# Storing attention's results by feature, with the reciprocals of their sums, and multiplying the two in the next stage: a decoder layer on one Trainium2 core

## The reference, cut to what matters

```python
# B = 4, S = 512, D = 256, 16 heads of 16, 160 experts, top 8
weights = softmax(einsum('bqhd,bkhd->bhqk', q, k) * 16 ** -0.5)
out = einsum('bhqk,bkhd->bqhd', weights, v)
x = layernorm(x + out.reshape(B, S, D) @ w_o.T)          # attention
x = layernorm(x + cross_attention(x, ctx_1024))          # "the mix"
x = layernorm(x + mixture_of_experts(x))                 # routed + shared expert
```

## Time and profile before

| | |
|---|---|
| median of 3 runs | 1057.27 us |
| the profiled execution | 1051.34 us, of which the span is 1049.5 us |
| attention | 0 to 287 us; its even part, 91.4 to 247.4 us, has PE busy for 154.6 of 156 us, DVE for 122.9, ACT for 110.4 |
| the mix | 287 to some 630 us |
| the experts and the end | some 630 to 1049.5 us |
| granted PE clock | 1.00 of full speed in the even part of attention, 0.83 in 285 to 345 us, 0.85 from 620 us on |
| DMA share | 0.78 in the even part of attention, 0.14 in 285 to 345 us |

### The profile page before, as it was taken

The page is one execution under the profiler, slowest core; times in us unless marked ns, Lnnn a source line. Parts: engine busy times, 40 slices in busy tenths (PEclk is TensorE's granted clock), DMA queues, the critical chain, the costliest instruction groups (busy, mean ns, idle before and its releaser), DMA issues. The chain is left out here.

```text
span 1049.5 us, 14995 instructions
## 1 busy us (share of the span) xinstructions
PE 805.3 (77%) x3800; PEld 533.6 (51%) x3800; DVE 492.6 (47%) x1287; ACT 381.8 (36%) x809; POOL 358.2 (34%) x360
## 2 busy tenths in 40 slices
PE   8989999999778898297484013888888887886295
PEld 4654444444246556174263012666666665765274
DVE  2778778777142576256424941222222222321077
ACT  3256777677623434215111000333333333332101
POOL 9101101110000014536265560555555555554200
PEclk9989999999969989698697555988989999887698
DMA  7998777885511022222122226888898887883296
GB/s 243 317 340 283 262 258 255 265 281 214 190 41 61 20 74 96 107 65 88 44 99 77 71 104 210 263 280 267 283 286 276 277 281 249 269 261 98 78 421 251
DMA packets 103410, 207.45 MB, mean 198 GB/s; under 512 B 25863, under 2 KB 51505, under 8 KB 97088
## 3 DMA queue, kind: packets, MB, share of 16 engines
q1 hardware_dynamic: 64160, 128.94, 37.1%
q10 hardware_dynamic: 24320, 42.74, 12.3%
q0 software_dynamic: 14880, 35.17, 9.2%
HBM read 117.76 MB, written 96.08 MB: 204 GB/s over the span
## 5 line engine op out<-in xcount | busy, mean ns | idle before, releaser
L1735 POOL DMA_INDIRECT contributions<-c_c,e_dest x182 | 177.5, 975 | 186.9 <-ACT c_c L1716 132.2
L1883 POOL DMA_INDIRECT row_pool<-rows,places x128 | 127.9, 999 | 210.8 <-issue 156.6
L1690 DVE COPY e_xt<-e_psx 128x256 f32<-128x256 f32 (+1 forms) x130 | 67.4, 530 | 250.7 <-PE e_psx L1622 106.3
L1636 PE MATMUL e_psg<-e_xt,e_w 128*128 128x64 f32 (+2 forms) x676 | 134.8, 339 | 51.8 <-ACT e_g L1709 40.4
L539 DVE TENSOR_REDUCE a_mx<-a_psS 128x2 f32<-128x1024 f32 x128 | 152.0, 1218 | 30.6 <-PE a_psS L361 30.4
L497 ACT ACTIVATE a_e<-a_psT 128x512 f32<-128x512 f32 x256 | 135.4, 600 | 56.4 <-PE a_psT L391 51.3
L1636 PEld LDWEIGHTS e_psg<-e_xt,e_w 128*128 128x128 f32 x676 | 109.7, 222 | 61.5 <-issue 48.8
L1709 ACT ACTIVATE e_g<-e_psg 128x128 f32<-128x128 f32 (+1 forms) x130 | 42.1, 324 | 243.4 <-PE e_psg L1636 132.3
L1647 PE MATMUL e_psy<-e_w,e_g 128*128 128x256 f32 (+1 forms) x442 | 121.4, 437 | 9.6 <-ACT c_c L1716 6.3
L1716 ACT ACTIVATE c_c<-e_psy,e_weight 128x256 f32<-128x256 f32 x182 | 80.7, 474 | 65.2 <-PE e_psy L1647 25.8
L391 PE MATMUL a_psT<-a_q,a_k 128*128 128x512 f32 x256 | 98.3, 451 | 4.6 <-ACT a_e L497 2.8
(11 more groups left out here) (284 smaller groups left out, 953.2 us busy)
## 6 DMA issues: line engine op xcount, KB each, us to landing
row_pool<-fill SPq DMA_DIRECT2D x32, 1260.0 KB, 7.2
e_w<-w ACTq DMA_DIRECT2D x156, 256.0 KB
rows<-row_pool SPq DMA_DIRECT2D x143, 140.0 KB
c_c<-contributions SPq DMA_DIRECT2D x16, 1024.0 KB, 17.1
a_k<-k_parts SPq DMA_DIRECT2D x64, 128.0 KB, 3.5
rows<-row_pool SPq DMA_DIRECT2D x78, 70.0 KB
a_q<-q_parts SPq DMA_DIRECT2D x32, 128.0 KB, 4.1
a_q<-q_parts SPq DMA_DIRECT2D x64, 64.0 KB, 3.4
```

Of the source, the lines that this page charges most:

```text
L1636: last = nc.tensor.matmul(ps_g(f, n)[:, k * own:(k + 1) * own], W[:, place, c * INTER:(c + 1) * INTER], XT[:, f.slot % XT_RING, at0:at0 + ...
L1690: nc.vector.tensor_copy(XT[:, at.slot % XT_RING, 0:n], ps_x(at, 0, n)).then_inc(xt_done, 1)
L1735: nc.gpsimd.indirect_dma_start(out=contrib, out_offset=bass.IndirectOffsetOnAxis(ap=dest[:, result(f) + k:result(f) + k + 1], axis=0), in_ ...
L1883: nc.gpsimd.indirect_dma_start(out=pool, out_offset=bass.IndirectOffsetOnAxis(ap=place[:, b, t, k:k + 1], axis=0), in_=rows[:, b, t], in_o ...
```

## The change

Attention no longer divides or turns its results. `turn_values`, the semaphores `o_turned` and `divided`, and the tiles `On` and `inv` are gone. DVE takes the reciprocal of the whole of `O` (128 x 512, features and sums alike) into a tile `Oinv`, after its second reduction. SP stores the rows of results of `O` and the rows of reciprocals of `Oinv` separately for each of four heads: eight DMAs of 16 rows of 2 KB in place of one. `O` is now held until these have landed. As bank 1 is free earlier, the banks are dealt anew: `BANK` skips it once, in place of twice, `rescore(6)` waits for the shifts, and the waits on exponentials follow from `BANK`.

```diff
-    BANK = [(k + (k >= 4) + (k >= 6)) % NT for k in range(NE)]
-    BEFORE = [None] * 3 + [0, 2, 3, 4, 5, None, 6, 7, 8, 9, 10, 11, 12]
+    BANK = [(k + (k >= 4)) % NT for k in range(NE)]
+    AFTER = 6
+    LAST_OF = [max(k for k in range(NE) if BANK[k] == n) for n in range(NT)]
+    BEFORE = [max((j for j in range(k) if BANK[j] == BANK[k]), default=None) for k in range(NE)]
+    STORES = 2 * HG
@@ SP, a step
-                    sp.wait_ge(divided, at.n - 2)
-                    cols = slice(g.slot * HG * DH, (g.slot + 1) * HG * DH)
-                    sp.dma_start(od[bass.ds(g.uses() - 1, 1), :, :, cols].rearrange("a p t e -> (a p) t e"),
-                                 On[:].rearrange("p t h e -> p t (h e)")).then_inc(stored, 16)
+                    for part, (src, done) in enumerate(((O, o_copied), (Oinv, inverted))):
+                        sp.wait_ge(done, at.n - 2)
+                        for hh in range(HG):
+                            at0 = 2 * DH * hh + DH * part
+                            sp.dma_start(od[bass.ds(g.uses() - 1, 1), part, g.slot, hh].rearrange("a e q -> (a e) q"),
+                                         src[at0:at0 + DH]).then_inc(stored, 16)
@@ PE
             def rescore(at, k):
-                (k < NT: waits on expd; BEFORE[k] None: waits on divided, or on the shifts)
+                if BEFORE[k] is not None:
+                    pe.wait_ge(expd, at.n * NE + BEFORE[k] + 1)
+                elif at.first():
+                    pe.wait_ge(v_done, B * TT)
+                else:
+                    pe.wait_ge(expd, (at.n - 1) * NE + LAST_OF[BANK[k]] + 1)
+                if k == AFTER and m.within(STEPS):
+                    pe.wait_ge(shifted0, m.n + 1)
+                    pe.wait_ge(shifted1, m.n + 1)
-            def turn_values(at):
-                for t in range(TT):
-                    last = nc.tensor.transpose(psT[:, TURNED, t * P:(t + 1) * P], O[:, t * P:(t + 1) * P], ident[:])
@@ ACT, copy_values
-                    act.wait_ge(o_turned, at.n)
+                    act.wait_ge(stored, 16 * STORES * at.n)
@@ DVE
-            def divide(at):
-                nc.vector.reciprocal(inv[:], o[:, :, :, DH]).then_inc(inverted, 1)
-                nc.vector.tensor_tensor(On[:], o[:, :, :, 0:DH], repeated(inv[:], 3, DH), ALU.mult).then_inc(divided, 1)
+            def invert(at):
+                dve.wait_ge(o_copied, at.n + 1)
+                if not at.first():
+                    dve.wait_ge(stored, 16 * STORES * at.n)
+                nc.vector.reciprocal(Oinv[:], O[:]).then_inc(inverted, 1)
-                    if at.back(3).within(STEPS) and i == 2:
-                        divide(at.back(3))
+                    if at.back(3).within(STEPS) and i == 1:
+                        invert(at.back(3))
```

```diff
     def load_heads(self, sp, o):
-        sp.dma_start(self.O[:], o).then_inc(self.o_in, 16)
+        for to, part in ((self.O[:].rearrange("p t d -> p (t d)").rearrange("p (c q) -> p c q", c=DC), 0), (self.OT[:], 1)):
+            sp.dma_start(to, o[part].rearrange("(c g) h e q -> (g h e) c q", c=DC)).then_inc(self.o_in, 16)
@@ DVE
+            def divide_heads(b):
+                dve.wait_ge(o_in, 32 * (b + 1))
+                for c in range(DC):
+                    nc.vector.tensor_tensor(OT[:, c], heads[:, c], OT[:, c], ALU.mult).then_inc(ot_done, 1)
             def start(b):
+                divide_heads(b)
                 measure_heads(b)
@@ DVE, a step
                 if part_c:
                     keep()
+                if part_a:
+                    divide_heads(n + 1)
                 if part_b:
                     statistics(...)
```

More of the change, by code:

```diff
@@ L275, in step @@
                     prefetch(sp)
-                    sp.wait_ge(stored, 16 * (STEPS - 2))
+                    sp.wait_ge(stored, 16 * STORES * (STEPS - 2))
                     first_heads(sp)
             run(sp, step)
-            sp.wait_ge(stored, 16 * STEPS)
+            sp.wait_ge(stored, 16 * STORES * STEPS)
         @block.gpsimd
@@ L376, in rescore @@
             def rescore(at, k):
[L377 to L383, removed]
+                m = at.back(-1)
+                if BEFORE[k] is not None:
                     pe.wait_ge(expd, at.n * NE + BEFORE[k] + 1)
-                elif g.within(STEPS):
-                    pe.wait_ge(divided, g.n + 1)
-                else:
+                elif at.first():
+                    pe.wait_ge(v_done, B * TT)
+                else:
+                    pe.wait_ge(expd, (at.n - 1) * NE + LAST_OF[BANK[k]] + 1)
+                if k == AFTER and m.within(STEPS):
                     pe.wait_ge(shifted0, m.n + 1)
@@ L404, in weigh @@
                 last.then_inc(weighed, 1)
-            def turn_values(at):
[L407 to L413, removed]
-                for t in range(TT):
-                    last = nc.tensor.transpose(psT[:, TURNED, t * P:(t + 1) * P], O[:, t * P:(t + 1) * P], ident[:])
-                last.then_inc(o_turned, 1)
             def step(at):
@@ L441, in step @@
                         weigh(g, TT - 1)
-                    if ending and i == 2:
-                        turn_values(g)
                     if finishing and i in (3, 5, 7):
@@ L514, in split @@
                                         ALU.subtract).then_inc(lo_done, 1)
-            def divide(at):
-                dve.wait_ge(o_turned, at.n + 1)
+            def invert(at):
+                dve.wait_ge(o_copied, at.n + 1)
                 if not at.first():
-                    dve.wait_ge(stored, 16 * at.n)
-                o = psT[:, TURNED].rearrange("p (t h e) -> p t h e", t=TT, h=HG)
-                nc.vector.reciprocal(inv[:], o[:, :, :, DH]).then_inc(inverted, 1)
-                dve.wait_ge(inverted, at.n + 1)
-                nc.vector.tensor_tensor(On[:], o[:, :, :, 0:DH], repeated(inv[:], 3, DH), ALU.mult).then_inc(divided, 1)
+                    dve.wait_ge(stored, 16 * STORES * at.n)
+                nc.vector.reciprocal(Oinv[:], O[:]).then_inc(inverted, 1)
             def shift(at):
@@ L684, in mix @@
         O, o_in = inputs.O, inputs.o_in
-        OT = sb("m_ot", [P, DC, S])
+        OT, heads = inputs.OT, O[:].rearrange("p t d -> p (t d)").rearrange("p (c q) -> p c q", c=DC)
         X1, X1b = (sb(f"m_{n}", [P, TT, D]) for n in ("x1", "x1b"))
@@ L750, in load_a @@
             def load_a(b):
[L752 removed]
+                sp.wait_ge(projected, TT * b)
                 inputs.load_heads(sp, od[b])
[L754 removed]
                 sp.dma_start(X[:], x[b]).then_inc(x_in, 16)
@@ L827, in turn @@
                 last.then_inc(done, 1)
-            def turn_heads(b):
-                pe.wait_ge(o_in, b * 16 + 16)
-                turn(O, 0, o_turned)
             def project_heads(b):
-                pe.wait_ge(ot_done, b + 1)
+                pe.wait_ge(ot_done, DC * (b + 1))
                 pe.wait_ge(x_in, b * 16 + 16)
@@ L964, in step @@
                 for t in range(TT):
-                    if t == 1 and part_a:
-                        turn_heads(n + 1)
                     nc.tensor.matmul(h[:, t], ident, X1b[:, t], start=True, stop=False)
@@ L1000, in _ @@
             w2, w3 = Cols[:, 0:DC], Cols[:, DC:2 * DC]
-            def copy_heads(b):
-                act.wait_ge(o_turned, b + 1)
-                for c in range(DC):
-                    last = nc.scalar.activation(OT[:, c], ps[:, c], ACT.Copy)
-                last.then_inc(ot_done, 1)
             def copy_x1(b):
@@ L1861, in decoder_layer @@
     qd, kd = (dram(n, [STEPS // 2, 2, DH, HG, 2, S]) for n in ("q_parts", "k_parts"))
-    od = dram("o_heads", [B, P, TT, D])
+    od = dram("o_heads", [B, 2, NG, HG, DH, S])
     pool = dram("row_pool", [POOL_ROWS, ROW])
```

14 lines of the change are left out of this document (4 added, 10 removed).

## The result

The changed kernel takes 1093.47 us (median of 4 runs, 1092.63 to 1096.54), the kernel before in the same comparison 1057.12 us (1056.08 to 1058.54). The ratio is 1.035, 95% interval 1.033 to 1.037: slower by 36 us. The forecast was 1108 us, in a range of 1075 to 1134.

The account below looks back on a forecast made before the run. PE was taken to pace attention, DVE having a fifth of its time spare. Attention's 48 us, plus 6 for the seam, less 2.6 in the mix, made 51 us on 1057.3: 1108 us, range 1075 to 1134.

Parts of the forecast that it names:

- The bound and the place: Attention: DVE's reciprocal ahead of six reductions delays score 4, leaving PE idle at least 2.4 us a step.
- The law of the step: Attention: a step grows by the reciprocal's time less 1.5 us, once that is above 1.5; 2.5 us expected.
- The size of R: Attention, DVE: the 512-element reciprocal's duration, taken as 4.0 us, with bounds of 0.69 and 7.8 us.
- the prediction's slow case: Whole kernel: reciprocal of 3.4 to 5.0 us and clock loss of 0 to 2 us a step, 1088 to 1132 us.
- The rival on the faster side: Attention and mix: reciprocal fast and stores hidden, 7.5 and 2.6 us won, seam costs 3: 1050 us; chance 0.13.
- The clock: Attention: idle PE brings a 3.5 us stretch at the lower clock, costing 1.2 us a step; bounds 0 and 2.5.
- The rival in which the clock holds: Attention: PE's gaps don't lower the clock, 32.5 us lost in place of 48: 1093 us; chance 0.13.
- The stores: Attention, SP: seven more stores at 0.65 us add some 4.6 us, 14.1 in all, hidden in a 17.8 us step.
- The second rival: Attention, SP: fast reciprocal, eight stores make SP the bound, steps of 14.1 to 16.2 us, 1057 to 1085 us; chance 0.12.
- The seam: Attention's end to the mix's first projection: 4 us later start plus 3 for multiplications, less 1 gained: 6 us.
- a wait put at nothing: Attention, ACT: its wait for eight stores, issued the step before and landing in some 2.4 us, costs nothing.
- The mix and what follows: Mix's other batches: eight transpositions leave PE's path three times, 0.87 us each, winning 2.6 us.

Follow-up runs that it names:

- v_one: Changed kernel with the reciprocals moved from attention to the mix, one 256 KB store a step and 16 loads a batch: 896.36 us, ratio 0.981 to the kernel before.
- v_r512: v_one with an unread reciprocal of 512 columns put back into each attention step behind the second reduction: 1072.82 us, ratio 1.021 to the kernel before.
- v_r384: v_one with an unread reciprocal of 384 columns put back into each attention step: steps of 15.12 us, ratio 1.000 to the kernel before.
- after_again: The changed kernel run once more, unaltered, beside other variants: 1089.13 us, ratio 1.035 to the kernel before.
- v_eight: v_one with the changed kernel's eight 32 KB stores a step and its two loads a batch: 916.17 us, ratio 1.002 to the kernel before.
- v_issue: v_one with seven more stores a step, each of one 2 KB row that nothing reads: 909.76 us, 11.0 above v_one.
- a_last: Changed kernel with separate tiles for the last group's results and reciprocals, so its copy waits for no store: 1087.78 us beside 1089.13 of after_again.
- v_r256: v_one with an unread reciprocal of 256 columns put back into each attention step: steps of 14.32 us, ratio 0.990 to the kernel before.

## Why the prediction was right, and where it was off

**The bound and the place.** "It is the place of the reciprocal, ahead of six reductions, that hurts, before its sum does": PE's idle bracket in a step is at score 4, released by L524 (L539 of the kernel before), as written. v_one, without the reciprocal, keeps PE busy for 107.99 of 110 us, and v_r512 brings the bracket back alone. The transpositions that went were worth 0.47 us a step there, 0.58 in the prediction.

**The law of the step.** "Longer by R - 1.5 us": with the measured R of 3.34 it gives 14.14 + 1.84 = 15.98, and 15.92 was measured at full clock. The three sizes give the same law: 1.74 - (14.32 - 14.14) = 1.56 us are free against the kernel before, and 2.54 and 3.34 us give 1.56 too.

**The size of R** was the term that missed most: 4.0 us were taken, 3.34 measured, 6.5 ns an element. The line through the earlier trace rows had 7.2 ns; pieces of 128, 256, 384 and 512 columns (926, 1736, 2536 and 3337 ns) give 6.3. Thirteen times 0.66 are 8.6 us; attention's 48 us became 40.2. R even lies below the 3.4 to 5.0 us that the prediction's slow case was spanned with; its lower end, 1088 us, doesn't come out of its own terms either (13 x 1.9 + 6 - 2.6 is 28 us, which gives 1085). The Trainium skill's VectorE: DVE Perf Modes, section "First, the fixed hardware budget", read as eight cycles an element, gives an estimate of 4.3 us. The trace has 3.34, nearer to that than to 0.7 us, the estimate from one element a cycle, which is a reading of Vector Engine (DVE) Microarchitecture Reference, section "3.2 Anatomy of a single slice". The rival on the faster side stood on that reading.

**The clock.** 1.2 us a step were taken, from a stretch of 3.5 us; 1.36 us were measured, in ten steps of twelve, over such a stretch. The rival in which the clock holds gave 1093 us, the time that came out, but the trace refutes it: the clock fell, and that its number was met is luck, as other terms were smaller. In v_r384, with gaps of 1.00 to 1.09 us, the clock did hold.

**The stores.** An issue cost 0.47 us, not 0.65 (four take 1.93 and 1.84 us, on SP's timeline), and they were hidden under the long step, as the prediction said; v_r512 against after_again shows it. The second rival's mechanism is real, but decides only with a short reciprocal: it was v_eight's 20 us. The Trainium skill's DMA: Bandwidth & Descriptors, section "Rules for kernel authors", wants small transfers coalesced. The runs agree: one, four and eight stores gave 896 to 899, 901 and 916 us, on two of the faster chips. v_issue adds that the number of issues counts and not only their size.

**The seam.** 6 us were summed, 8.3 measured. From the last copy's start to ACT's first work in the mix: 7.49 us for 4.86, 2.6 more where 4 was written. R is 0.7 us of that difference, and from the last issue's end to ACT's start it takes 1.8 us where 2.4 and 0.35 were written. From there to `project_heads`' first matmul: 6.73 for 3.51, 3.2 where 3 was written. The steps of the tail gain 0.95 us, where 1 was written (the last copy starts 20.84 us behind the last shift in a_last, 21.79 in the kernel before). Missing is the wait for stores, 3.4 us (24.21 less 20.84). "They are issued in the step before and land in some 2.4 us, so it is behind them" holds in the even part and fails in the last step, where the queue carries the mix's inputs as well. That is the step of the prediction that failed: a wait put at nothing, by a landing time taken from a stretch with another queue.

**The mix and what follows** won 7.3 us where 2.6 was written. The multiplications fell into the gap named (1.91 us are left of 4.25, in after_again), and the matmuls that surround it run unbroken. The first two batches won 2.3 us, from matmul to matmul (106.1 for 108.3), but 4.6 in after_again (103.8), so the 2.6 can be neither confirmed nor denied. The third won 7.6 us (61.3 for 69.0), and what follows lost 2.6 (583.0 for 580.4). In that stretch DVE and ACT wait for something that no engine releases, which the trace calls remote. DVE's waits for it ahead of `m_g`, from 400 to 650 us, first before, then after:

```profile
DVE m_g L1421 <- remote: 20.4, 2, 14.9
```

```profile
DVE m_g L1395 <- remote: 10.6, 1, 10.6
```

In after_again it is 28.4 us in two waits. On the slower chips the third batch took 69.0, 61.3, 68.5, 61.3 and 68.6 us in the five kernels before, changed, after_again, v_r512 and v_r256. The changed kernel and after_again are the same program. So these 7 us move without any edit, and what sets them isn't shown. Behind the seam the changed kernel won 7.3 us and after_again 6.6, but in different batches, so how much of it the edits gave is open.

**From the profile to the median.** The two profiled executions lie 41.3 us apart, the medians 36.4. The kernel before was profiled in a run that was 6 us below its median, the changed one in its fastest. The forecast put the profile's difference on the median; 4.9 of its 14.5 us are that. The others: attention 7.8 and the mix 4.7 too high, the seam 2.3 too low, which makes 10.2; the 0.6 between is the rounding of the sum and of the median it was put on.

The second run of the same program, after_again, has its last shift at 296.83 us, 4.1 us earlier than the changed kernel: three of its steps had more of the upper clock (13.55, 15.94 and 15.47 us for 14.76, 17.26 and 16.79). So attention's loss is 36 to 40 us. The seam came out alike (8.4 us). The time fell well inside the range because the main mechanism was right; all terms but the seam were put too high.

## What to carry to other kernels

Reciprocals belong on the compact form: the kernel before took 16 elements a partition where the new one takes 512, sixteen copies of each sum and all results with them, and in DVE's order whatever stands behind that waits. The layout itself pays once the reciprocals stand where DVE has time and one store carries everything: v_one is faster than the kernel before by 1.9%, and v_eight gives that back by issuing eight. The time that a DMA takes to land in the even part can't be carried over to the last step, where other transfers stand ahead of it.

## What the runs showed of the hardware

- A reciprocal on DVE costs 6.3 to 6.5 ns an element: 926 ns for 128x128, 3337 ns for 128x512. A power on GpSimd took 82160 ns for 128x512.
- Gaps of 1.00 to 1.09 us in PE's work in every step left the clock at its upper level (v_r384). Gaps of 1.79 to 1.91 us were followed by about 3.5 us near the lower one, at 1.36 us a step, in ten of twelve steps of the changed kernel, and in nine of twelve of after_again and of v_r512 the step was as much longer.
- Seven stores of one 2 KB row each took 2.86 us of SP's time (0.41 us each, where one of 32 KB took 0.49), and 11 us of the kernel's. Where SP went on without a pause, loads issued right behind two fills of 1260 KB took up to 1.2 to 1.3 us to issue in place of 0.56.
- Four stores of 32 KB landed 7.8 us behind the last issue with 12 loads of about 5 MB issued ahead of them; the median of such stores is 1.6 to 2.0 us.
- The kernel before took 1054 to 1057 us in two comparisons and 914 to 915 us in three others, on chips 1, 8 and 2. Between v_r256 (slower) and v_r384 (faster) the first two batches of the mix agree (53.2 and 50.5 us, 52.6 and 50.5), the third takes 68.6 and 50.7 us, and what follows 575.5 and 457.9. So these two executions differ by chip from the third batch on.
